# Who rounds the attention weights of steps 1, 27 and 29: VectorE in place of ScalarE, in a graph layer with quadratic attention

## The chip, the cores and the metric

The kernel runs on one core of a Trainium2 chip. The metric is the device time of one execution in microseconds (us), and below it is the median of several executions. The kernel is written by hand in the instruction language: every engine has its own program, and the engines meet at semaphores alone.

## The reference

The layer takes 1250 nodes of 768 features and 20,000 edges. After a layer norm `xn` it adds a graph convolution and an attention without softmax, and behind that a switch feed-forward with 8 experts. What the change touches is the attention, 12 heads of 64:

```python
q, k, v = qkv[0] * SCALE, qkv[1], qkv[2]
A = jnp.einsum('bhnd,bhmd->bhnm', q, k)
numerator = 1.0 + A + 0.5 * A * A
attn = numerator / numerator.sum(axis=-1, keepdims=True)
out = jnp.einsum('bhnm,bhmd->bhnd', attn, v)
```

Since 1 + A + A²/2 = ((1 + A)² + 1)/2, the kernel squares 1 + A on ScalarE, adds 1, and divides by sums that it gets in another way. Products are made in single precision from pairs of rounded numbers: a value is split into a rounded high part (type fp32r) and the low rest, and TensorE multiplies both.

## The kernel before

The twelve heads are done as six pairs, one pass of a loop for each. Five passes run in a hardware loop (`for j in Fori(0, PAIRS - 1)`), the sixth stands behind it (`turn(PAIRS - 1, True)`) without the work for a next pair. A pass has 30 steps: 2 heads by 3 chunks of some 416 queries by 5 pairs of key tiles of 125 nodes. For step `i` in a pass:

- TensorE makes the scores of both key tiles (`MQ` by `KH` and `KL`, lines 1130 and 1131), four matmuls. I call these scores i.
- ScalarE squares 1 + scores into `Pf` (line 815, ACT `Pf<-ps`).
- Either ScalarE (line 793) or VectorE (line 1003) rounds `Pf` + 1 into the high part `Ph`. The list `HI_ON_ACT` (line 593) says which.
- VectorE makes the low part `Pl` = `Pf` + 1 - `Ph` (line 1005).
- Three steps later (`LAG`) TensorE multiplies `Ph` and `Pl` by the values (line 1146, four matmuls). I call this value product i. It waits for `p_lo`, which counts the low parts.

`Pf`, `Ph` and `Pl` are rings of three (`RING`): the square of step i waits for the low part of i-3, and whoever writes `Ph` or `Pl` of step i for value product i-3. VectorE and ScalarE execute what stands in their programs in order. ScalarE issues the rounding of step i-1 behind the square of step i, VectorE does the rounding of step i right ahead of the low part of step i:

```python
if HI_ON_ACT[i]:
    dve.wait_ge(p_hiA, j * NA + (sum(HI_ON_ACT[:i]) + 1))
else:
    dve.wait_ge(sq_done, j * STEPS + (i + 1))
    dve.tensor_scalar(h, f, 1.0, None, ALU.add).then_inc(p_hiD, 1)
    dve.wait_ge(p_hiD, j * ND + (i - sum(HI_ON_ACT[:i]) + 1))
```

Between the steps stands other work, placed by step numbers (`READ_AT`, `TURN_AT`, `FIRST_AT` and the like). What matters here of VectorE's:

- at the start of a pass: lower parts of keys and queries (line 875 `KLB`, line 879 `MA`) and a quadratic form (line 923, `R`), in steps 0 to 9;
- in steps 6 to 22 of the five passes in the loop: 20 comparisons of edge keys (line 958, `eqp`), whose results GpSimd scatters into the matrix `counts` (line 365);
- at the end of a pass: the low part of three groups of transposed keys (line 889, `kt`) at i = 26, 29 and 32, two sums of halves (line 936, `OUN`), and the finish of the pair's output (lines 946, 949, 950, `R`, `OHL`) at i = 30, 32 and 35.

TensorE projects keys and queries for the next pair meanwhile (lines 1873 to 1875, in slices), transposes its keys (line 1069) at i = 24, 27 and 30, where the second and third group wait for VectorE's `kt` of the group before, and at i = 32 makes the Gram matrix of the keys (line 1076), which waits for the third `kt`. Then the next pass begins.

ScalarE at i = 28 has, behind the square of step 28: the rounding of step 27, a copy of half an output (line 802, `tmpo`), a read of queries (line 751, `Q`), the high part of the second key group (line 767, `kt`), then the square of step 29 and the rounding of step 28.

Of the kernel before, what the change touches and what calls it, by code (L numbers as in the profile page):

```python
# [68 lines left out]
STEPS = 30  # L69
# [30 lines left out]
def build(nc, x, src, dst, gnn_w, gnn_b, w_qkv, b_qkv, w_proj, b_proj, sw, sb_, w1, b1, w2, b2, out,  # L100
          counts, keyd, vdram, odram, xfd, x1d, invd):
    ctx = ExitStack()
    with ctx:
# [486 lines left out]
                    pe.wait_ge(xt_lo, FIRST_UNIT[4])  # L590
                value(i)

        HI_ON_ACT = [i % 5 in (1, 3) or i in (0, 27, 29) for i in range(STEPS)]
        NA = sum(HI_ON_ACT)
        ND = STEPS - NA
        FREE = 1
# [140 lines left out]
        def _(act):  # L737
# [48 lines left out]
            def turn(j, last):  # L786
                def round_weights(i):

                    w = step(i)[4]
                    act.wait_ge(sq_done, j * STEPS + (i + 1))  # L790
                    if i >= RING:
                        act.wait_ge(pv_done, j * STEPS + (i - RING + 1))
                    act.activation(Ph[:, i % RING, :, 0:w], Pf[:, i % RING, :, 0:w], ACT.Identity,  # L793
                                   bias=1.0).then_inc(p_hiA, 1)
# [14 lines left out]
                for i in range(END):  # L809
                    if i < STEPS:  # L810
                        w = step(i)[4]
                        act.wait_ge(sc_done, j * STEPS + (i + 1))
                        if i >= RING:
                            act.wait_ge(p_lo, j * STEPS + (i - RING + 1))
                        act.activation(Pf[:, i % RING, :, 0:w], ps[0:T, 2 * (i % 2):2 * (i % 2) + 2, 0:w],  # L815
                                       ACT.Square, bias=1.0).then_inc(sq_done, 1)
                    if 1 <= i <= STEPS and HI_ON_ACT[i - 1]:
                        round_weights(i - 1)
# [40 lines left out]
        def _(dve):  # L859
# [56 lines left out]
            def turn(j, last):  # L916
# [61 lines left out]
                for i in range(END):  # L978
# [15 lines left out]
                    if i < STEPS:  # L994
                        w = step(i)[4]
                        p, f, h = Pl[:, i % RING, :, 0:w], Pf[:, i % RING, :, 0:w], Ph[:, i % RING, :, 0:w]
                        if i >= RING:
                            dve.wait_ge(pv_done, j * STEPS + (i - RING + 1))
# [6 lines that stand above are left out]
                        dve.scalar_tensor_tensor(out=p, in0=f, scalar=1.0, in1=h.bitcast(F32), op0=ALU.add,  # L1005
# [899 lines left out]
```

## Time and profile before

| | |
|---|---|
| median of 3 executions | 1080.57 us (1078.35 to 1081.0) |
| the profiled execution | 1076.3 us, its span 1074.5 us |
| TensorE busy | 928.6 us, 86% of the span |
| VectorE busy | 778.9 us, 72% |
| ScalarE busy | 482.1 us, 45% |
| GpSimd busy | 352.3 us, 33% |
| chain that ended last, by engine | PE 55%, DVE 19%, issue 11%, ACT 6%, DMA 5% |

PE is TensorE's matmuls, PEld its weight loads, DVE VectorE, ACT ScalarE, POOL GpSimd. The six passes lie at 139 to 615 us of the span; a pass in the loop takes 82 us. The span is counted from the first to the last instruction, and the execution's own time is 1.8 us more.

### The profile page before, as it was taken

The page shows a single profiled execution, that of the slowest core. Times are in us where ns is not written, and L with a number is a line of the kernel's source. Part 1 is how long each engine was busy: PE and PEld are TensorE (multiplying, and loading weights), DVE is VectorE, ACT ScalarE, POOL GpSimd, SP SyncE. Part 2 cuts the span into 40 slices and gives each one's busy share as a digit, 9 for nine tenths or more (in the row PEclk, how much of TensorE's full clock was granted, in tenths as well). Part 3 has the DMA queues.
Part 4 walks back from the last instruction along what each step waited for, and adds up shares of the span by engine and source line. Part 5 has one row for each costly group of instructions (what it writes and reads, how often), then busy time and mean ns, then how long its engine had stood idle before and what let it go on. Part 6 is the DMA issues. An engine that isn't in the chain of part 4 may idle for free.

```text
span 1074.5 us, 15640 instructions
## 1 busy us (share of the span) xinstructions
PE 928.6 (86%) x5294; PEld 884.8 (82%) x5294; DVE 778.9 (72%) x1553; ACT 482.1 (45%) x710; POOL 352.3 (33%) x233
## 2 busy tenths in 40 slices
PE   2896799999999999999998679789999996498985
PEld 2896788888888888888887579789999996398885
DVE  6869169888889889889888825665666767467673
ACT  2311266666666766766767402111323223165640
POOL 2025556544545545545345000000000001435562
PEclk9998899999999999999999989989999996589998
DMA  9966452472462462472353194465556533568761
GB/s 278 338 163 152 78 109 19 73 145 29 72 141 33 72 137 36 72 144 29 72 87 91 47 175 119 105 155 145 143 155 159 153 116 130 145 194 265 244 219 46
DMA packets 137406, 136.65 MB, mean 127 GB/s; under 512 B 70361, under 2 KB 118076, under 8 KB 136337
## 3 DMA queue, kind: packets, MB, share of 16 engines
q1 hardware_dynamic: 109550, 119.23, 42.1%
q0 software_dynamic: 27408, 16.66, 10.1%
q8 instruction: 26, 0.43, 0.2%
q10 hardware_dynamic: 403, 0.17, 0.1%
q14 instruction: 19, 0.16, 0.1%
HBM read 94.27 MB, written 38.14 MB: 123 GB/s over the span
## 4 chain that ended last, share of the span: by engine, by line
PE 55%; DVE 19%; issue 11%; ACT 6%; DMA 5%; POOL 1%; SPq 1%; DVEq 0%; ACTq 0%; POOLq 0%
PE ps L1873 13%; PE ps L1874 12%; PE ps L1875 12%; PE ps L1146 6%; DVE Pl L1005 3%; PE ps L1130 3%; PE ps L1131 3%; DVE Ph L1003 3%; DMA out<-oE,ids 2%; ACT Ph L793 2%; ACT Pf L815 2%; PE ps L1512 1%; DVE eqp L958 1%; DMA Cs<-counts 1%; PE ps L1106 1%
## 5 line engine op out<-in xcount | busy, mean ns | idle before, releaser
L365 POOL DMA_INDIRECT counts<-countc,idxu x157 | 269.0, 1713 | 289.8 <-DMA counts<-countc,idxu 197.6
L1005 DVE SCALAR_TENSOR_TENSOR Pl<-Pf,Ph 125x832 fp32r<-125x832 f32 (+1 forms) x180 | 184.0, 1027 | 51.3 <-ACT Ph L793 47.4
L815 ACT ACTIVATE Pf<-ps 125x832 f32<-125x832 f32 (+1 forms) x180 | 156.0, 867 | 129.7 <-PE ps L1131 120.0
L1146 PE MATMUL ps<-Ph,vsb 125*128 125x416 f32 (+1 forms) x360 | 131.2, 365 | 22.6 <-DVE Pl L1005 22.5
L1146 PE MATMUL ps<-Pl,vsb 125*128 125x416 f32 (+1 forms) x360 | 126.7, 352 | 0.0
L1146 PEld LDWEIGHTS ps<-Ph,vsb 125*128 125x128 f32 x360 | 67.7, 188 | 36.0 <-DVE Pl L1005 21.2
L1873 PE MATMUL ps<-wH,XH 128*125 128x384 f32 x240 | 84.3, 351 | 9.9 <-DVE OHL L950 5.8
L1873 PE MATMUL ps<-XH,wqkH 128*128 128x416 f32 (+1 forms) x216 | 83.0, 384 | 9.8 <-DVE wqkL L862 8.1
L1874 PE MATMUL ps<-wL,XH 128*125 128x384 f32 x240 | 83.0, 346 | 0.0
L1875 PE MATMUL ps<-wH,XL 128*125 128x384 f32 x240 | 82.8, 345 | 0.0
L793 ACT ACTIVATE Ph<-Pf 125x832 fp32r<-125x832 f32 (+1 forms) x90 | 80.5, 896 | 0.7
L1874 PE MATMUL ps<-XL,wqkH 128*128 128x416 f32 (+1 forms) x216 | 77.4, 358 | 0.0
L1875 PE MATMUL ps<-XH,wqkL 128*128 128x416 f32 (+1 forms) x216 | 77.3, 358 | 0.0
L1873 PE MATMUL ps<-HH,CH 125*125 125x384 f32 x200 | 69.3, 346 | 7.3 <-DVE CL L1345 7.3
L1146 PEld LDWEIGHTS ps<-Pl,vsb 125*128 125x128 f32 x360 | 68.1, 189 | 0.7
L1874 PE MATMUL ps<-HL,CH 125*125 125x384 f32 x200 | 68.3, 342 | 0.0
L1875 PE MATMUL ps<-HH,CL 125*125 125x384 f32 x200 | 68.3, 341 | 0.0
L1130 PE MATMUL ps<-MA,KHA 128*125 128x416 f32 (+1 forms) x180 | 66.2, 368 | 1.8 <-DVE MA L879 1.8
L1130 PE MATMUL ps<-MB,KHB 128*125 128x416 f32 (+1 forms) x180 | 64.9, 361 | 0.0
L1131 PE MATMUL ps<-MA,KLA 128*125 128x416 f32 (+1 forms) x180 | 63.6, 354 | 0.0
L1651 POOL MEMSET xe<- 105x1536 f32 x1 | 1.4, 1382 | 189.5 <-DVE lg L1349 189.5
L1131 PE MATMUL ps<-MB,KLB 128*125 128x416 f32 (+1 forms) x180 | 63.3, 352 | 0.0
(254 smaller groups left out, 2276.3 us busy)
## 6 DMA issues: line engine op xcount, KB each, us to landing
Cs<-counts SPq DMA_DIRECT2D x20, 546.9 KB
w1s<-L_ffn_w SPq DMA_DIRECT2D x8, 1152.0 KB, 6.1
w2s<-L_ffn_w SPq DMA_DIRECT2D x8, 1152.0 KB, 5.7
odram<-OHL SPq DMA_DIRECT2D x12, 625.0 KB, 7.7
oS<-odram SPq DMA_DIRECT2D x10, 750.0 KB, 4.8
vdram<-VS SPq DMA_DIRECT2D x10, 672.0 KB
vsb<-vdram SPq DMA_DIRECT2D x12, 560.0 KB
kt<-keyd SPq DMA_DIRECT2D x5, 1280.0 KB, 6.0
```

Of the source, the lines that this page charges most:

```text
L365: pool.indirect_dma_start(out=counts, out_offset=bass.IndirectOffsetOnAxis(ap=idxu[:, c:c + 1], axis=0), in_=countc[:, c:c + 1], in_offset ...
L793: act.activation(Ph[:, i % RING, :, 0:w], Pf[:, i % RING, :, 0:w], ACT.Identity, bias=1.0).then_inc(p_hiA, 1)
L815: act.activation(Pf[:, i % RING, :, 0:w], ps[0:T, 2 * (i % 2):2 * (i % 2) + 2, 0:w], ACT.Square, bias=1.0).then_inc(sq_done, 1)
L958: ins = dve.scalar_tensor_tensor(out=eqp[:, s % 2, :], in0=keys_of, scalar=kcur[:, s:s + 1], in1=triw[:, m0:m0 + WINDOW * P], op0=ALU.is_e ...
L1003: dve.tensor_scalar(h, f, 1.0, None, ALU.add).then_inc(p_hiD, 1)
L1005: dve.scalar_tensor_tensor(out=p, in0=f, scalar=1.0, in1=h.bitcast(F32), op0=ALU.add, op1=ALU.subtract).then_inc(p_lo, 1)
L1130: pe.matmul(out_, KH[a][:, kt * T:(kt + 1) * T], q, start=True, stop=False)
L1131: ins = pe.matmul(out_, KL[a][:, kt * T:(kt + 1) * T], q, start=False, stop=True)
L1146: ins = pe.matmul(ps[:, 4 + s % 2, 0:w], vsb[:, 2 * kp + t, a, :], part[:, m % RING, t, 0:w], start=(kp == 0 and t == 0 and part is Ph), s ...
L1873: pe.matmul(out, lh, rh, start=(k == 0), stop=False)
L1874: pe.matmul(out, lh, rl, start=False, stop=False)
L1875: ins = pe.matmul(out, ll, rh, start=False, stop=(k == tiles - 1))
```

## The change

The list that names the steps whose weights ScalarE rounds:

```diff
-        HI_ON_ACT = [i % 5 in (1, 3) or i in (0, 27, 29) for i in range(STEPS)]
+        HI_ON_ACT = [i % 5 in (1, 3) and i != 1 or i == 0 for i in range(STEPS)]
         NA = sum(HI_ON_ACT)
         ND = STEPS - NA
```

Before, ScalarE rounds steps 0, 1, 3, 6, 8, 11, 13, 16, 18, 21, 23, 26, 27, 28, 29 of a pass (15) and VectorE the other 15. Now steps 1, 27 and 29 are VectorE's: 12 and 18, in all six passes. Shapes, buffers and results are the same.

VectorE at the start of a pass in the loop, from the low part of query keys behind step 0 to the low part of step 1:

```order
 L879 TENSOR_TENSOR MA<-Q,MA 64x416
-L1000 REGISTER_ALU
+L1002 ISA
+L1003 TENSOR_SCALAR Ph<-Pf 125x836
+L1004 ISA
 L1005 SCALAR_TENSOR_TENSOR Pl<-Pf,Ph 125x836
 L874 REGISTER_ALU
 L875 TENSOR_TENSOR KLB<-K,KHB 64x418
```

The rounding of step 1 has come in between two instructions of VectorE; the program waits for the square there where it waited for ScalarE's rounding.

VectorE at the end of a pass in the loop, from the keys' low part at i = 26 over the low parts of steps 27 and 28 (left out between) to that of step 29:

```order
 L875 TENSOR_TENSOR KLA<-K,KHA 64x416
+L1002 REGISTER_ALU
+L1003 TENSOR_SCALAR Ph<-Pf 125x2x416
+L1004 REGISTER_ALU
 L1005 SCALAR_TENSOR_TENSOR Pl<-Pf,Ph 125x2x416
...
+L1000 REGISTER_ALU
 L1005 SCALAR_TENSOR_TENSOR Pl<-Pf,Ph 125x2x416
 L889 TENSOR_TENSOR kt<-ps,kt 125x4x128
 L998 REGISTER_ALU
+L1002 REGISTER_ALU
+L1003 TENSOR_SCALAR Ph<-Pf 125x2x416
+L1004 REGISTER_ALU
 L1005 SCALAR_TENSOR_TENSOR Pl<-Pf,Ph 125x2x416
```

Step 27's rounding stands ahead of its low part now, and step 29's between the keys' low part and the last `Pl` of the pass. The register instructions work out the values that the waits compare with; a pass of the loop has 95 of them on VectorE where it had 79.

ScalarE in the same place, behind the squares of steps 28 and 29:

```order
 L815 ACTIVATE Pf<-ps 125x2x416
-L793 ACTIVATE Ph<-Pf 125x2x416
 L802 ACTIVATE tmpo<-ps 64x416
...
 L762 ACTIVATE MA<-Q 64x418
-L793 ACTIVATE Ph<-Pf 125x2x416
 L766 REGISTER_ALU
 L767 ACTIVATE kt<-ps 125x2x128
```

Two roundings are gone, the first of them ahead of everything that ScalarE does up to the rounding of step 28.

## Rows read from the trace of the kernel before

**Rows 1.** third pass: us, busy PE, PEld, DVE, ACT, POOL, clock, DMA share, GB/s

```profile
302.40:384.30 81.90, 76.48 (x405) 71.64 (x404) 71.38 (x138) 54.63 (x80) 45.66 (x27) 1.00 0.46 84
```

**Rows 2.** TensorE's waits, 140 to 630 us: us, times, longest

```profile
PE ps L1146 <- DVE Pl L1005: 22.5, 25, 2.0
PE ps L1069 <- DVE kt L889: 9.4, 8, 1.7
PE ps L1873 <- DVE OHL L950: 5.8, 1, 5.8
```

**Rows 3.** groups by line, 180 to 760 us: busy us, mean ns | idle before

```profile
L1003 DVE TENSOR_SCALAR Ph<-Pf 125x832 fp32r<-125x832 f32 x54 | 33.1, 612 | 4.1 <-DVE eqp L958 1.4 <-PE ps L1146 0.9
L793 ACT ACTIVATE Ph<-Pf 125x832 fp32r<-125x832 f32 x56 | 50.0, 894 | 0.3
```

**Rows 4.** time line, start of the third pass: start, us, engine, instruction [idle before]

```profile
308.82 1.07 DVE L1005 SCALAR_TENSOR_TENSOR Pl<-Pf,Ph 125x836 fp32r<-125x836 f32 x1 [1.10 <-ACT Ph L793]
311.74 1.97 DVE L1005 SCALAR_TENSOR_TENSOR Pl<-Pf,Ph 125x836 fp32r<-125x836 f32 x2
311.75 0.90 ACT L793 ACTIVATE Ph<-Pf 125x836 fp32r<-125x836 f32 x1
312.83 0.46 PE L1146 MATMUL ps<-Ph,vsb 125*128 125x418 f32 x1 [0.90 <-DVE Pl L1005]
```

**Rows 5.** time line, the same pass, step 10

```profile
329.62 0.58 DVE L1003 TENSOR_SCALAR Ph<-Pf 125x832 fp32r<-125x832 f32 x1
330.23 1.03 DVE L1005 SCALAR_TENSOR_TENSOR Pl<-Pf,Ph 125x832 fp32r<-125x832 f32 x1
331.41 0.43 PE L1146 MATMUL ps<-Ph,vsb 125*128 125x416 f32 x1 [1.25 <-DVE Pl L1005]
```

**Rows 6.** time line, the same pass, step 5 on VectorE

```profile
316.24 0.60 DVE L1003 TENSOR_SCALAR Ph<-Pf 125x832 fp32r<-125x832 f32 x1
316.87 1.02 DVE L1005 SCALAR_TENSOR_TENSOR Pl<-Pf,Ph 125x832 fp32r<-125x832 f32 x1
```

**Rows 7.** time line, end of the second pass: VectorE

```profile
291.01 1.03 DVE L1005 SCALAR_TENSOR_TENSOR Pl<-Pf,Ph 125x832 fp32r<-125x832 f32 x1 [1.01 <-ACT Ph L793]
294.24 1.03 DVE L1005 SCALAR_TENSOR_TENSOR Pl<-Pf,Ph 125x832 fp32r<-125x832 f32 x1 [1.46 <-ACT Ph L793]
295.18 0.68 DVE L889 TENSOR_TENSOR kt<-ps,kt 125x512 fp32r<-125x512 f32 x1
295.78 1.02 DVE L1005 SCALAR_TENSOR_TENSOR Pl<-Pf,Ph 125x832 fp32r<-125x832 f32 x1
299.75 0.42 DVE L889 TENSOR_TENSOR kt<-ps,kt 125x256 fp32r<-125x256 f32 x1
```

**Rows 8.** time line, end of the second pass: ScalarE and TensorE

```profile
292.46 0.87 ACT L815 ACTIVATE Pf<-ps 125x832 f32<-125x832 f32 x1
293.20 0.91 ACT L793 ACTIVATE Ph<-Pf 125x832 fp32r<-125x832 f32 x1
290.39 0.35 PE L1131 MATMUL ps<-MB,KLB 128*125 128x416 f32 x1
295.92 0.48 PE L1069 MATMUL ps<-ident,K 128*125 128x128 f32 x2 [1.66 <-DVE kt L889]
300.22 1.46 PE L1076 MATMUL ps<-kt 125*128 125x256 f32 x10
```

**Rows 9.** time line, end of the last pass

```profile
603.71 1.95 DVE L1005 SCALAR_TENSOR_TENSOR Pl<-Pf,Ph 125x832 fp32r<-125x832 f32 x2
606.58 1.96 DVE L1005 SCALAR_TENSOR_TENSOR Pl<-Pf,Ph 125x832 fp32r<-125x832 f32 x2 [0.91 <-ACT Ph L793]
615.47 0.65 PE L1873 MATMUL ps<-wH,XH 128*125 128x384 f32 x1 [5.85 <-DVE OHL L950]
```

**Rows 10.** VectorE's rounding, all 90 (ns min/median/max); GpSimd's last scatter

```profile
L1003 DVE TENSOR_SCALAR Ph<-Pf x90: 532/595/899, 149.0 to 600.5; 125x832 fp32r<-125x832 f32 x60, 125x836 fp32r<-125x836 f32 x30
585.66 1.55 POOL L365 DMA_INDIRECT counts<-countc,idxu  x1 [0.30 <-issue]
```

## The prediction

> **What bounds the kernel now.** I read the busy times by stage first, then TensorE's waits, then the time line around the three steps. In one pass of the loop TensorE is busy 76.5 of 81.9 us at a granted clock of 1.00, VectorE 71.4, ScalarE 54.6, GpSimd 45.7 [rows 1]. So TensorE sets the pace and stands still some 5.4 us a pass. The view of waits says for what: over all passes 22.5 us for low parts `Pl`, 9.4 us for the low part `kt` of transposed keys, 5.8 us once for `OHL` behind the last pass [rows 2]. All three are VectorE's. VectorE is nearly full, and where it stands still it mostly waits for a rounding of ScalarE. A rounding takes ScalarE 894 ns and VectorE 612 ns [rows 3]. So the change gives VectorE 0.6 us of work where it may have been waiting for 0.9 us of ScalarE's. Whether that pays is a matter of each place: what ends the next wait.
>
> The price on VectorE is the spacing from the start of a rounding to the start of its low part: 0.61 us in step 10, 0.63 us in step 5 [rows 5, 6]. I take 0.62.
>
> **Step 1.** VectorE waited 1.10 us for ScalarE before the low part of step 1, so it was free at 308.82 - 1.10 = 307.72 [rows 4]. The square of step 1 was done by then: ScalarE made it ahead of the rounding of step 0, which VectorE had already used. With its own rounding VectorE starts the low part at 307.72 + 0.03 + 0.62 = 308.37, 0.45 us earlier. The two small operations behind it, the rounding of step 2 and the low part of step 2 follow without a wait, 0.45 us earlier as well. TensorE waited 0.90 us for that low part (value product 2, at 312.83 [rows 4]), so it goes on 0.45 us earlier.
>
> But this is lent, not given. The low parts of steps 2 and 3 stand as one row of 1.97 us from 311.74, so it ends at 313.71, and the second, 1.03 us long, starts at 312.68 [rows 4]. ScalarE's rounding of step 3 ends at 311.75 + 0.90 = 312.65 [rows 4]. It follows the squares of steps 3 and 4 and two other operations, and the scores of step 3 come before TensorE's wait, so it doesn't move. VectorE therefore waits 0.45 us there and starts the low part of step 3 when it did before. From there to step 10 VectorE has no wait on another engine that the trace shows, and TensorE's next stop is for the low part of step 10: VectorE ends it at 330.23 + 1.03 = 331.26, and TensorE starts at 331.41 after 1.25 us [rows 5]. That time stays, and the 0.45 us are waited there. The other four passes of the loop and the last have the same stop at step 10. So step 1 is worth 0 in all six passes. What hides it is VectorE's backlog from step 3 to 10; without that it would give 6 x 0.45 = 2.7 us.
>
> **Step 27 in the loop.** VectorE waited 1.01 us before the low part of step 27, so it was free at 290.00 [rows 7]. Its own rounding gives 290.00 + 0.62 = 290.62 against 291.01, about 0.4 us earlier. More matters on ScalarE: with 0.90 us less ahead of it, the square of step 29 moves from 292.46 to 291.56, and the rounding of step 28 from 293.20 to 292.30 [rows 8]. The scores of step 29 are no obstacle, their last matmul ends at 290.39 + 0.35 = 290.74 [rows 8], 0.8 us before. VectorE waited 1.46 us before the low part of step 28 [rows 7], and was free at 292.78, now at 292.4; so the low part starts 0.90 us earlier, at 293.34. The keys' low part moves from 295.18 to 294.28, and TensorE's transposes, which waited 1.66 us for it, from 295.92 to 295.02 [rows 7, 8].
>
> **Step 29 in the loop.** VectorE rounds it behind `kt`, with nothing to hide it: 0.62 us. The low part of step 29 comes at 295.78 - 0.90 + 0.62 = 295.50, 0.28 us earlier. Up to the third `kt` VectorE runs on but for a wait of 0.16 us on itself. That `kt` ended at 299.75 + 0.42 = 300.17, and the Gram matrix started at 300.22 [rows 7, 8], so VectorE is what it waits for. TensorE would be there 0.9 us earlier but gets 0.28. The next pass starts that much earlier, for both engines, since VectorE waits 1 us for step 0 there. The five ends of loop passes show the same waits to 0.1 us. Sum: 5 x 0.28 = 1.4 us gained.
>
> **Steps 27 and 29 in the last pass.** There the square of step 29 waits for the low part of step 26, by the ring of three, and ScalarE's rounding of step 28 comes behind it: neither moves. The rounding of step 27 goes between the two low parts of the row at 603.71, which ends at 605.66; the second then ends at 606.28, still before 606.58 [rows 9]. The idle 0.91 us cover it: 0. The rounding of step 29 goes between the two at 606.58 [rows 9], and from there VectorE runs on through `OHL` to the start of the next stage at 615.47 [rows 9]: 0.62 us lost.
>
> **Small things.** A pass has 16 more register instructions on VectorE. Step 10 has one between rounding and low part already, step 5 none, and the spacings are 0.61 and 0.63 us [rows 5, 6]: I take 0. As an upper bound I take the 0.02 to 0.03 us between the end of a rounding and the start of what waits for it, 16 x 5 x 0.03 = 2.4 us. TensorE's and GpSimd's programs are unchanged, and no DMA moves.
>
> **Sum.** -1.4 + 0.6 = -0.8 us: the profiled execution would take 1075.5 instead of 1076.3 us. It lies 4.3 us under the median of the runs, so for the median I forecast 1080.57 - 0.8 = 1079.8 us. A measurement of this kernel can tell about 0.3% from no change, 3.2 us: this isn't told.
>
> **The rivals.**
>
> *The roundings lie open in the tail (slower).* If the rounding of step 28 does not come earlier, because something else holds ScalarE's square of step 29, then `kt` stays and step 29's 0.62 us go onto VectorE's chain to the Gram matrix in each pass, as they do in the last. 6 x 0.62 = 3.7 us: 1084.3 us; at the longest rounding, 0.90 us, it is 5.4 us. It decides as soon as the gain at step 28 is below 0.62 us. Against it: the 0.8 us that the scores are early. Chance 0.08.
>
> *The tail isn't the last wait (faster).* If TensorE, not `kt`, sets the start of the Gram matrix, each of five passes keeps 0.90 us, and if the backlog at step 10 dissolves too, 0.45 us in six: 4.5 + 2.7 - 0.6 = 6.6 us, 1074.0 us. For it: TensorE is the busiest. Against it: 0.05 us between the end of `kt` and the Gram matrix [rows 7, 8]. Chance 0.08.
>
> *GpSimd holds up VectorE's roundings.* The 90 roundings take 532 to 899 ns [rows 10]; the 14 above 650 ns all overlap one of GpSimd's scatter instructions, of the 36 that overlap none not one is. The excess is 0.3 us at most, and 14 of 54 give 0.06 us on average, which is within my 0.62. If a rounding had to wait for the rest of a scatter instruction, half of 1.55 us [rows 10] in 45.7/81.9 = 0.56 of the cases [rows 1], each would cost 0.43 us more: step 29's gain of 0.28 turns into a loss of 0.15 in five passes, and the sum is 0.8 + 0.6 = +1.4 us, 1082.0 us. Chance 0.12. The Trainium skill's page SBUF — State Buffer, section "SBUF: two separate sides", speaks for this rival: it calls the port pair that VectorE and GpSimd share an exclusive lock, kept for the whole instruction, while the loser fully blocks. The measured excess is smaller than that rule read strictly would give. GpSimd itself could be slowed, but its last scatter starts at 585.66 [rows 10], 30 us before the stage that needs it.
>
> *The register instructions count*: up to +2.4 us, 1082.2 us. Chance 0.10.
>
> **How the numbers follow.** The forecast has the remaining 0.62. Three of the five cases lie within 0.3% (1077.3 to 1083.8 us). Lower end of the range: step 1's 2.7 us stay, 1077.1, less 1.1 us of scatter (the runs differ by 2.65 us): 1076.0. Upper end: 1082.2 plus 1.3 us: 1083.5. Faster by over 0.3%: 0.08 and some scatter, 0.11. Slower: 0.08 and as much, 0.11. Same: 0.78.
>
> **What would show it.** TensorE's wait for the low part of step 2 falls from 0.90 to 0.45 us, and that at step 10 rises from 1.25 to 1.7 us. VectorE's wait before `Pl` of steps 1 and 27 is gone, that before step 28 is about 1 us. TensorE's wait for the second `kt` falls from 1.66 to 1.2 us, and a wait of 0.8 us for the third `kt` appears. The distance from pass to pass falls by 0.3 us, and the last pass ends 0.6 us later against its start. I am wrong if the wait at step 10 stays 1.25 us, if the third `kt` comes later than before, or if the passes change by over 0.5 us.

## The result and the profile after

| | before | the change |
|---|---|---|
| median of 8 executions each, same chip | 1081.43 us (1077.41 to 1085.76) | 1088.81 us (1081.97 to 1095.09) |
| ratio | | 1.0056 [1.0028, 1.0083] |
| the profiled execution | 1076.3 us | 1081.97 us |
| its span, mean granted clock | 1074.5 us, 0.952 | 1080.2 us, 0.942 |

The change is 0.56% slower. The forecast was 1079.8 us and "not told from no change", and the range ended at 1083.5 us. Two further measurements of the same kernel, told below, gave ratios of 1.0012 and 1.0020. In two of the three the interval lies above no change, so there is a loss, but its size differs from one measurement to the next. The ratios and their 95% intervals are worked out from all executions and are not the quotient of the medians. One execution of all that follow, of e5, took 1559.73 us at a mean clock of 0.557, and its ratio and mean clock are those of the other eleven.

First the terms of the forecast, in the order of its steps. The third pass of the change begins at 305.04 us, 2.6 us later than before. Its time line at steps 1 to 3, VectorE and then TensorE's value product of step 2 (start, us, engine, instruction [idle before <-releaser]):

```profile
310.42 0.59 DVE L1003 TENSOR_SCALAR Ph<-Pf 125x836 fp32r<-125x836 f32 x1
311.05 1.03 DVE L1005 SCALAR_TENSOR_TENSOR Pl<-Pf,Ph 125x836 fp32r<-125x836 f32 x1
...
315.49 1.03 DVE L1005 SCALAR_TENSOR_TENSOR Pl<-Pf,Ph 125x836 fp32r<-125x836 f32 x1 [0.54 <-ACT Ph L793]
...
315.01 0.46 PE L1146 MATMUL ps<-Ph,vsb 125*128 125x418 f32 x1 [0.43 <-DVE Pl L1005]
```

The wait of 1.10 us ahead of the low part of step 1 [rows 4] is gone, and TensorE waits 0.43 us at step 2 in place of 0.90. VectorE then waits 0.54 us for ScalarE's rounding of step 3, where the forecast had 0.45. The end of the second pass, VectorE and then TensorE:

```profile
292.90 0.58 DVE L1003 TENSOR_SCALAR Ph<-Pf 125x832 fp32r<-125x832 f32 x1
...
296.27 1.03 DVE L1005 SCALAR_TENSOR_TENSOR Pl<-Pf,Ph 125x832 fp32r<-125x832 f32 x1 [0.98 <-ACT Ph L793]
297.21 0.68 DVE L889 TENSOR_TENSOR kt<-ps,kt 125x512 fp32r<-125x512 f32 x1
297.81 0.58 DVE L1003 TENSOR_SCALAR Ph<-Pf 125x832 fp32r<-125x832 f32 x1
...
302.40 0.42 DVE L889 TENSOR_TENSOR kt<-ps,kt 125x256 fp32r<-125x256 f32 x1
...
297.95 0.48 PE L1069 MATMUL ps<-ident,K 128*125 128x128 f32 x2 [1.19 <-DVE kt L889]
...
302.88 1.46 PE L1076 MATMUL ps<-kt 125*128 125x256 f32 x10 [0.66 <-DVE kt L889]
```

The waits are where the forecast had them. VectorE waits 0.98 us before step 28 (forecast about 1, before 1.46 in [rows 7]), TensorE 1.19 us for the second `kt` (1.2, before 1.66 in [rows 8]), and the Gram matrix has a new wait of 0.66 us (0.8). The last pass takes 71.23 us up to the next stage against 70.89 before, 0.34 us more (forecast 0.62).

One sign came out the other way. In the third pass, which has no disturbance in either kernel, the third `kt` should come earlier in the pass. Time lines of VectorE, the third `kt` before and in the change:

```profile
380.19 0.42 DVE L889 TENSOR_TENSOR kt<-ps,kt 125x256 fp32r<-125x256 f32 x1
...
383.12 0.42 DVE L889 TENSOR_TENSOR kt<-ps,kt 125x256 fp32r<-125x256 f32 x1
```

The pass began at 302.40 before and begins at 305.04 now, so the third `kt` comes after 77.79 us before and after 78.08 in the change, 0.29 us later, and the pass takes 80.72 us where it took 80.44. In the fifth pass it is 0.32 us earlier. Undisturbed passes of the kernel before take 80.44 to 81.28 us, so a term of 0.3 us a pass can't be read from two of them.

TensorE's waits over all passes, 135 to 640 us (in total, times, longest), to set beside [rows 2]:

```profile
PE ps L1146 <- DVE Pl L1005: 20.1, 25, 2.0
PE ps L1069 <- DVE kt L889: 6.4, 7, 1.2
PE ps L1873 <- DVE OHL L950: 5.8, 1, 5.8
...
PE ps L1076 <- DVE kt L889: 3.5, 5, 0.9
```

TensorE waits 2.4 us less for low parts, 3.0 us less at the transposes, and 3.5 us more at the Gram matrix: in sum less than before. And yet the span is 5.7 us longer. Where it went shows when the passes are laid side by side. These are passes 2 to 5 of the change, and the second pass cut up from step 10 (us, busy PE, PEld, DVE, ACT, POOL, clock, DMA share, GB/s):

```profile
221.68:305.04 83.36, 78.13 (x397) 73.07 (x396) 71.80 (x138) 50.84 (x75) 41.03 (x24) 0.96 0.47 79
305.04:385.76 80.72, 75.20 (x397) 70.15 (x396) 72.86 (x139) 50.95 (x75) 43.71 (x25) 1.00 0.47 82
385.76:469.00 83.24, 78.14 (x397) 73.09 (x396) 71.92 (x139) 50.83 (x75) 42.09 (x25) 0.96 0.46 79
469.00:549.72 80.72, 75.11 (x397) 70.12 (x396) 72.52 (x139) 50.83 (x75) 43.94 (x26) 1.00 0.48 82
250.00:252.00 2.00, 1.09 (x8) 1.11 (x8) 2.00 (x4) 1.12 (x2) 1.27 (x1) 1.00 0.10 0
252.00:253.00 1.00, 1.00 (x8) 1.00 (x7) 0.88 (x4) 0.81 (x2) 0.02 (x1) 0.53 0.21 0
253.00:258.00 5.00, 5.00 (x16) 4.76 (x17) 2.52 (x5) 1.15 (x2) 1.65 (x1) 0.50 0.21 20
258.00:259.00 1.00, 1.00 (x8) 1.00 (x6) 0.35 (x1) 0.62 (x1) 0.00 (x0) 0.55 0.35 2
259.00:261.00 2.00, 2.00 (x13) 1.97 (x13) 1.76 (x4) 0.00 (x0) 0.00 (x0) 1.00 0.35 57
```

Passes 3 and 5 take 80.72 us at a granted clock of 1.00. (The stretch of 81.90 us in [rows 1] is not one pass: the third pass before ends at 382.84, and takes 80.44 us. The 82 us told ahead of the prediction are the mean of all five, of which the first takes 86.22.) Passes 2 and 4 hold the same 397 matmuls and take 83.36 and 83.24 us, with 2.9 us more of PE busy time and a clock of 0.96. The finer rows find the place. From 252 to 259 us the granted clock is 0.50, which is 1.2 GHz, the lower of TensorE's two levels, and then it is back at 1.00. TensorE is busy all that time. What it did before stands in its time line:

```profile
250.91 0.43 PE L1146 MATMUL ps<-Ph,vsb 125*128 125x416 f32 x1 [1.84 <-DVE Pl L1005]
...
251.75 1.37 PE L1106 MATMUL ps<-blocks,R 128*125 128x2 f32 x8
...
253.47 0.55 PE L1874 MATMUL ps<-XL,wqkH 128*128 128x416 f32 x1
253.82 0.55 PE L1875 MATMUL ps<-XH,wqkL 128*128 128x416 f32 x1
...
259.49 0.35 PE L1874 MATMUL ps<-XL,wqkH 128*128 128x416 f32 x1
259.68 0.35 PE L1875 MATMUL ps<-XH,wqkL 128*128 128x416 f32 x1
```

It stood still for 1.84 us at the value product of step 10, up to 250.91. Then the same matmuls start 0.35 us apart at the lower level and 0.19 us apart at the higher. The wait was 1.25 us before [rows 5], and the forecast had it grow to 1.7. It did so in every pass of the loop (here 1.76 to 1.90 us), but not in the last, where it is 1.12 us and was 1.16. Behind two of the five it was followed by a fall of the clock; behind 1.90 us in pass 3 it was not:

```profile
334.34 0.43 PE L1146 MATMUL ps<-Ph,vsb 125*128 125x416 f32 x1 [1.90 <-DVE Pl L1005]
```

So the 5.7 us of span are made up as follows. The two passes with a fall are 2.64 and 2.52 us over 80.72, +5.2 us. The rest of the five passes is -0.7 us: they take 414.1 us, 409.0 with the two at 80.72, against 409.7 before (forecast -1.4). The last pass is +0.34, and what lies ahead of the first and behind the last is +0.9. In the execution shown of the kernel before, no pass of the loop has such a fall.

Whole spans of single executions can't be compared as finely as passes. What lies behind the last pass is the same program in all kernels here, and it took 455.3 to 461.6 us in the fourteen profiles, with TensorE at half clock for 77 to 88 us of it.

### The profile page after: what moved, and what is told of

Same layout as the page of the kernel before. It is cut to its first block, busy times and chain, and to the rows that moved or that the text cites. A ratio compares the mean times of both kernels' runs of the same rounds, so it can differ in the third digit from the quotient of the medians.

```text
span 1080.2 us, 15678 instructions
## 1 busy us (share of the span) xinstructions
PE 938.5 (87%) x5294; PEld 894.8 (83%) x5294; DVE 788.2 (73%) x1571; ACT 467.1 (43%) x692; POOL 356.3 (33%) x233
## 4 chain that ended last, share of the span: by engine, by line
PE 54%; DVE 18%; issue 13%; DMA 6%; ACT 5%; POOL 1%; SPq 1%; DVEq 1%; ACTq 0%; POOLq 0%
PE ps L1873 12%; PE ps L1874 12%; PE ps L1875 12%; PE ps L1146 5%; DMA out<-oE,ids 3%; DVE Ph L1003 3%; PE ps L1130 3%; PE ps L1131 3%; DVE Pl L1005 3%; ACT Ph L793 2%; DMA xe<-xfd,ids 1%; PE ps L1106 1%; PE ps L1512 1%; DVE eqp L958 1%; DMA Cs<-counts 1%
## 5 line engine op out<-in xcount | busy, mean ns | idle before, releaser
L365 POOL DMA_INDIRECT counts<-countc,idxu x157 | 274.0, 1745 | 287.4 <-DMA counts<-countc,idxu 212.3
L1003 DVE TENSOR_SCALAR Ph<-Pf 125x832 fp32r<-125x832 f32 (+1 forms) x108 | 66.6, 617 | 4.9 <-DVE eqp L958 1.1
L793 ACT ACTIVATE Ph<-Pf 125x832 fp32r<-125x832 f32 (+1 forms) x72 | 64.5, 896 | 0.6
```

What stands on the lines that cost most here:

```text
L365: pool.indirect_dma_start(out=counts, out_offset=bass.IndirectOffsetOnAxis(ap=idxu[:, c:c + 1], axis=0), in_=countc[:, c:c + 1], in_offset ...
```

## The experiments

Two theories stood at the start. **Clock:** the work is worth what was forecast, and the longer wait at step 10 now and then brings a fall of the clock; then filling that wait with work gets the loss back, though TensorE does more. **Work:** VectorE's three more roundings, or the new wait at the Gram matrix, cost the time; then filling changes nothing or makes it worse. In the expectations, theory A is the first; rival B is the new wait at the Gram matrix, by its length or by falls of its own, and rival C is VectorE's work.

All times are medians, beside runs of the kernel before on the same chip. The mean clock is that of the executions of a row, over their whole span; that of the kernel before was 0.943 over 65 executions in all, and in its profiled execution 0.952.

| kernel | edits | median us (n) | before us | ratio | mean clock |
|---|---|---|---|---|---|
| e1 | step 1 alone | 1083.1 (12) | 1082.84 | 1.0017 [0.9995, 1.0039] | 0.941 |
| e2 | steps 27 and 29 alone | 1079.94 (12) | 1082.84 | 0.9964 [0.9943, 0.9985] | 0.944 |
| e3 | the change, wait at step 10 filled (8) | 1075.18 (6) | 1082.84 | 0.993 [0.9907, 0.9953] | 0.947 |
| e4 | the kernel before, filled (5) | 1077.65 (8) | 1082.84 | 0.995 [0.993, 0.9969] | 0.948 |
| e5 | the change, wait at Gram filled (3) | 1085.86 (12) | 1081.94 | 1.0032 [1.0004, 1.0059] | 0.938 |
| e6 | the change, step 7 to ScalarE | 1076.23 (6) | 1081.94 | 0.994 [0.9917, 0.9964] | 0.945 |
| e7 | 27 and 29, filled (5) | 1073.38 (6) | 1081.94 | 0.9918 [0.9892, 0.9944] | 0.949 |
| e8 | the change again | 1082.8 (12) | 1081.94 | 1.0012 [0.9992, 1.0032] | 0.940 |
| e9 | 27 and 29, step 7 to ScalarE | 1074.73 (6) | 1080.99 | 0.9935 [0.9915, 0.9956] | 0.946 |
| e10 | e9, filled (3) | 1071.59 (6) | 1080.99 | 0.9904 [0.9882, 0.9926] | 0.949 |
| e11 | the change, filled (4) | 1074.99 (6) | 1080.99 | 0.9941 [0.992, 0.9962] | 0.948 |
| e12 | the change a third time | 1082.84 (12) | 1080.99 | 1.002 [1.0001, 1.004] | 0.941 |

### The parts of the change: e1 and e2

e1 moves step 1 alone, e2 steps 27 and 29 alone:

```diff
-        HI_ON_ACT = [i % 5 in (1, 3) or i in (0, 27, 29) for i in range(STEPS)]
+        HI_ON_ACT = [i % 5 in (1, 3) and i != 1 or i in (0, 27, 29) for i in range(STEPS)]
```

```diff
-        HI_ON_ACT = [i % 5 in (1, 3) or i in (0, 27, 29) for i in range(STEPS)]
+        HI_ON_ACT = [i % 5 in (1, 3) or i == 0 for i in range(STEPS)]
```

> Only step 1's rounding goes to VectorE; 27 and 29 stay on ScalarE. Theory A (the clock after the stop at step 10): the 0.45 us of TensorE's wait move from step 2 to step 10, where it stands 1.7 to 1.9 us in one piece, and in some passes the granted clock then falls to 0.50 for 6.8 us, which costs 3 us each time. Expected 3 to 8 us slower than before, with a mean clock of 0.935 to 0.945, and more spread from run to run. Rival B (the tail: the new wait for the third kt brings the clock down or costs the time): no difference from before, within 1 us. Rival C (VectorE simply has too much work): a third of the loss, 2 us, with the clock as before.

> Only steps 27 and 29 go to VectorE; step 1 stays on ScalarE. Theory A: TensorE's wait at step 10 stays 1.25 us, no more falls of the clock than before, and the time is 0 to 2 us below before. Rival B: 5 to 7 us slower, the falls of the clock come with it. Rival C: 4 to 5 us slower with the clock as before.

Steps 27 and 29 make the kernel faster, by 0.36% (1.6 to 6.2 us by the interval), where 0 to 2 us were expected. Step 1 measured 0.17% slower, with an interval that includes no change. That is less than the 3 to 8 us that the clock theory had put on it, and no more than the 2 us of rival C, so e1 by its time alone doesn't tell the theories apart. The waits at step 10 were 1.77 to 1.85 us in e1 and 1.25 to 1.45 in e2. In the profiles e1 had falls behind four of its five waits. The first three passes of e1 by that wait, time lines of TensorE:

```profile
169.79 0.42 PE L1146 MATMUL ps<-Ph,vsb 125*128 125x416 f32 x1 [1.78 <-DVE Pl L1005]
250.57 0.43 PE L1146 MATMUL ps<-Ph,vsb 125*128 125x416 f32 x1 [1.83 <-DVE Pl L1005]
334.52 0.43 PE L1146 MATMUL ps<-Ph,vsb 125*128 125x416 f32 x1 [1.85 <-DVE Pl L1005]
```

e2 shows that a wait as long as the old one can bring a fall too. Its third pass, time line of TensorE:

```profile
330.63 0.43 PE L1146 MATMUL ps<-Ph,vsb 125*128 125x416 f32 x1 [1.25 <-DVE Pl L1005]
```

And windows of e2 ahead of that wait and behind it (columns as in the windows above, the clock is third from the right):

```profile
326.00:330.00 4.00, 3.38 (x18) 2.97 (x16) 3.87 (x10) 3.62 (x6) 1.75 (x2) 1.00 0.14 0
333.00:335.00 2.00, 2.00 (x7) 1.91 (x7) 2.00 (x3) 0.00 (x0) 0.76 (x1) 0.50 0.21 0
```

Three of e2's five passes have such a fall, and the kernel before, with waits of 1.24 to 1.38 us there, has none in the one execution shown. So the length of the wait does not decide it alone, and it is likely that the kernel before loses time in this way as well, only not in the execution that I had read. e4 tests that.

### Filling the wait: e3, e4, e11, and e7

TensorE makes matmuls into a bank that nobody reads at that point, in place of standing still. e3 has 8 on top of the change, e11 4, e4 has 5 on top of the kernel before:

```diff
+                        if m == 10:
+                            pe.wait_ge(r_done, 3 * j + 3)
+                            for _ in range(8):
+                                pe.matmul(ps[:, 6, 0:416], XH[:, 0, 0:P], XH[:, 0, 0:416], start=True, stop=True)
                         pe.wait_ge(p_lo, j * STEPS + (m + 1))
```

> The whole change, and at step 10 TensorE does 8 more matmuls, whose result nobody reads, in the time in which it waits for the low part of step 10. All of the reference's work is done. Theory A: the clock stays at 1.00 in all passes of the loop, and the time is that of before or up to 2 us less. Rivals B and C: no gain over the change, 5 to 8 us slower than before, or more.

> The kernel before, with 5 such matmuls in the wait of 1.25 us at step 10. Theory A: if some executions of the kernel before have falls of the clock at this place too, this one's median is 1 to 4 us below before and its spread smaller; if they never have, it is the same within 0.5 us. Rivals B and C: the same within 0.5 us.

> The whole change with 4 unread matmuls at step 10 instead of 8, so that about 1.0 us of the wait of 1.8 stays open. Theory A: between the change and the change filled, nearer to the filled one: 1075 to 1079 us, mean clock 0.944 to 0.947.

The change with the fill takes 0.993 of the time of the kernel before, with 48 more matmuls. TensorE's time line in e3's second pass:

```profile
249.66 1.75 PE L1146 MATMUL ps<-XH 128*128 128x416 f32 x8 [0.22 <-DVE R L923]
251.25 0.35 PE L1150 MATMUL ps<-Ph,vsb 125*128 125x416 f32 x1
```

Windows of e3 over the same place:

```profile
249.00:252.00 3.00, 2.78 (x15) 2.38 (x14) 2.97 (x6) 2.13 (x3) 0.45 (x1) 1.00 0.19 0
252.00:255.00 3.00, 3.00 (x21) 2.94 (x21) 2.84 (x6) 1.10 (x4) 0.00 (x0) 1.00 0.00 0
```

The wait is gone but for 0.22 us, and the clock stays at 1.00 where the change had 0.50, as it does in all five passes. e3 is 7.7 us below the kernel before, more than the 0 to 2 us expected. Eight matmuls are even too many, since the value product follows them without a wait; half of them (e11) did as well. The kernel before gains too, 0.5% (e4). That bears on a question that the forecast had not asked: why its median lay 4.3 us above the profiled execution. The mean clock over its executions, 0.943, is lower than the 0.952 of the profiled one, and the fill brings the median down to about what the profiled execution took. That its ordinary executions have falls in the loop follows from this gain; no profile of it shows one.

Then the good half of the change and the fill together, e7: steps 27 and 29 on VectorE, five unread matmuls at step 10.

> Steps 27 and 29 on VectorE, step 1 on ScalarE, and 5 unread matmuls in the wait of 1.25 us at step 10. If the 0.45 us of step 1 really are worth nothing, this is the same as the whole change filled: 1075 us, 7 us below before, within 1 us. If they are worth what they first give, it is 2 to 3 us above that.

With the falls in the loop out of the way the terms of the work can be read, from one execution each. Counted from the start of its pass, the second `kt` starts 0.88 to 1.02 us earlier in e7 than in e4 in passes 2 to 5 (forecast 0.90), and the third 0.03 to 0.39 us earlier (forecast 0.28). The five passes take 408.44 us in e4 and 406.86 in e7: 1.6 us, where the forecast had 1.4. But 0.6 us of it lie in the first pass, and e2, with the same three roundings, has 86.22 us there, exactly as before; the other four give 0.95 us.

The last pass takes 70.98 us in e4 and 71.02 in e7, but e4 has a fall of some 3.4 us in the midst of it and e7 has none, so these two don't price the roundings. (Every profile has one more fall at the end of this pass, while TensorE waits for `OHL`.) The nine profiles without a fall in its midst do, though some differ in steps 1 and 7 too: it takes 71.0 to 71.6 us in the seven with steps 27 and 29 on VectorE, and 70.7 and 70.9 us in the two with them on ScalarE (e1, before). That is some 0.5 us, near the 0.62 of the forecast.

In e3 and e11, which have step 1 on top of e7, the five passes take 408.06 and 408.21 us: 1.2 and 1.35 us more than in e7. Half of that is again the first pass, in which e7 is the short one. In the other four it is 0.1 to 0.2 us a pass, less than like passes differ. By the ratios it is 0.1 to 0.2% (0.993 and 0.9941 against 0.9918), within the intervals. So a price of step 1 beyond the falls isn't shown.

### A control: e5

If any work put into any wait helped, the fill at step 10 would prove little. e5 fills the change's other new wait, ahead of the Gram matrix, with three matmuls:

```diff
+                        for _ in range(3):
+                            pe.matmul(ps[:, 0, 0:416], XH[:, 0, 0:P], XH[:, 0, 0:416], start=True, stop=True)
```

> The whole change, and 3 matmuls whose result nobody reads in TensorE's new wait for the third kt, ahead of the Gram matrix, in the five passes of the loop; the wait at step 10 stays open. Theory A (the falls of the clock come from the wait at step 10): 3 to 8 us slower than before, as the change. Rival B (the new wait at the end of a pass brings them): as fast as before or faster, mean clock 0.945 or more.

It is 1.0032 [1.0004, 1.0059], as slow as the change itself. TensorE's waits in e5, 135 to 640 us:

```profile
PE ps L1146 <- DVE Pl L1005: 18.3, 20, 2.0
...
PE ps L1076 <- DVE kt L889: 0.6, 2, 0.3
```

And the place itself, time line of TensorE in e5 at the end of the second pass:

```profile
303.39 0.72 PE L1171 MATMUL ps<-XH 128*128 128x416 f32 x3
304.20 0.86 PE L1076 MATMUL ps<-kt 125*128 125x256 f32 x5
```

The wait at the Gram matrix is filled (0.6 us left of 3.5), the waits at step 10 are still 1.75 to 1.90 us in the loop, and there are three falls behind them. Of the new waits it is the one at step 10 that counts.

### Shortening the wait in place of filling it: e6, e9, e10

The wait at step 10 is VectorE's backlog. e6 takes 0.6 us of it away by giving the rounding of step 7 to ScalarE, on top of the change; e9 leaves step 1 on ScalarE too, and e10 is e9 with three unread matmuls at step 10:

```diff
-        HI_ON_ACT = [i % 5 in (1, 3) and i != 1 or i == 0 for i in range(STEPS)]
+        HI_ON_ACT = [i % 5 in (1, 3) and i != 1 or i == 0 or i == 7 for i in range(STEPS)]
```

```diff
-        HI_ON_ACT = [i % 5 in (1, 3) or i in (0, 27, 29) for i in range(STEPS)]
+        HI_ON_ACT = [i % 5 in (1, 3) or i in (0, 7) for i in range(STEPS)]
```

> The whole change, and in exchange step 7's rounding goes from VectorE to ScalarE, which is idle there. VectorE's backlog from step 3 to step 10 is 0.62 us shorter. Theory A: TensorE's wait at step 10 falls from 1.8 to about 1.2 us; the passes take 0.6 us less each, 3 us in all, and the falls of the clock are as rare as in the kernel before or rarer: 3 to 7 us faster than before. Rival C (VectorE has too much work): only the 3 us of work, 2 us slower to 1 us faster than before.

> A version that might beat both: steps 27 and 29 on VectorE, steps 1 and 7 on ScalarE, no unread matmuls. TensorE's wait at step 10 falls to 0.7 us. Theory A: no falls of the clock in the passes of the loop, mean clock 0.947 or more, 1070 to 1074 us, 8 to 12 us below before. If work alone counts: 3 to 4 us below the kernel with only 27 and 29 moved, 1076 us.

> The same with 3 unread matmuls in the wait of 0.7 us at step 10. Theory A: the short wait brings the clock down rarely, so this is the same within 1 us, or 1 to 2 us faster. If it is 3 us faster or more, even a wait of 0.7 us costs the clock.

e6 has waits of 1.13 to 1.27 us, one fall in its profile, and 0.994, 5.7 us below the kernel before. Some 3 us of that are work, 0.6 us of waiting less in each of five passes; the rest fits rarer falls. e9 has waits of 0.79 to 1.10 us and 0.9935. It was expected 8 to 12 us below the kernel before and without falls; it is 6.3 us below, and 3 us below e2 by the ratios, as much as was expected of the work alone. It has no fewer falls than e6 in its profile: one was there behind 1.10 us in the second pass. TensorE's time line of e9:

```profile
249.62 0.43 PE L1146 MATMUL ps<-Ph,vsb 125*128 125x416 f32 x1 [1.10 <-DVE Pl L1005]
```

Windows of e9 at the wait and behind it, where the clock is 0.57 on average:

```profile
248.00:250.00 2.00, 0.90 (x5) 0.57 (x4) 1.97 (x5) 1.80 (x3) 0.53 (x1) 1.00 0.21 0
251.00:254.00 3.00, 3.00 (x12) 2.87 (x12) 2.84 (x6) 0.53 (x2) 1.25 (x1) 0.57 0.19 0
```

e10 is 3.1 us faster than e9 on the same chip. The intervals overlap a little, but five of e9's six executions are slower than every one of e10's. So even this wait costs more than its length, and e10 is the fastest of all: 1071.59 us, 0.9904 [0.9882, 0.9926]. In its trace the fill and the rest of the wait are:

```profile
248.06 0.73 PE L1146 MATMUL ps<-XH 128*128 128x416 f32 x3
249.04 0.46 PE L1150 MATMUL ps<-Ph,vsb 125*128 125x416 f32 x1 [0.26 <-DVE Pl L1005]
```

### The change again: e8 and e12

> The changed kernel once more, with a second profile. Theory A: TensorE waits 1.8 us at step 10 in each pass of the loop, and falls of the clock begin within some 3 us around the end of that wait and nowhere else in the passes of the loop; 4 to 8 us slower than before. If the falls come at other places, or the loss is there without them, A is wrong.

> The changed kernel a third time, to fix the size: the first comparison gave 1.0056, the second 1.0012. Theory A: 1.001 to 1.005, with a mean clock of 0.936 to 0.941 against 0.943 of before, and the time of an execution falls by 0.4 us for each us less at half clock. A ratio below 0.999 would say that the slowdown was not the change's.

e8 came out less slow than expected, at 1.0012, with an interval that includes no change; e12 is at 1.002, within what was expected. Their waits at step 10 are 1.76 to 2.08 us and their profiles have three falls each, all behind that wait, as in every profile here: no pass of the loop has a fall at another place. The shorter kind of fall is in the third pass of e12, TensorE's time line:

```profile
331.00 0.42 PE L1146 MATMUL ps<-Ph,vsb 125*128 125x416 f32 x1 [1.91 <-DVE Pl L1005]
```

Windows of e12 from the wait on:

```profile
329.00:331.00 2.00, 0.09 (x2) 0.03 (x1) 1.97 (x4) 0.99 (x3) 0.89 (x1) 1.00 0.20 0
331.00:334.00 3.00, 3.00 (x18) 2.95 (x19) 2.84 (x7) 1.89 (x3) 2.15 (x2) 0.90 0.00 0
334.00:335.00 1.00, 1.00 (x5) 0.94 (x4) 1.00 (x2) 0.00 (x0) 1.00 (x1) 0.50 0.42 1
335.00:337.00 2.00, 2.00 (x9) 1.92 (x7) 0.85 (x3) 1.12 (x2) 1.00 (x1) 0.55 0.27 7
```

It lasts some 3.4 us where that of the change lasts 6.8, and such a pass takes 82.2 to 82.3 us, where one without a fall takes 80.15 in e12 and 80.72 in the change: 1.5 to 2.1 us. Over the three measurements the change has 32 executions, with a median of 1083.3 us, against 1081.9 us in 73 of the kernel before. Their mean clocks are 0.940 and, over the 65 for which it is known, 0.943. Among the 32, time and clock go together (correlation -0.89): 0.94 us for each 0.001 of mean clock. The mean clock counts every stage, so it doesn't say how much of this lies in the loop: of the 21.5 us at half clock that the profile of the change has more than that of the kernel before, 13.7 are the two falls and 7 lie behind the last pass.

## Why the prediction was wrong

**The step that failed** is the last of step 1: "That time stays, and the 0.45 us are waited there. [...] So step 1 is worth 0 in all six passes." The first half is right. But I treated 0.45 us of waiting at step 2 and 0.45 us more at step 10 as the same thing. At step 10 they lengthen a pause of 1.25 us to 1.8. I counted TensorE's waits as time and never asked what a pause does to the clock of the work behind it; a granted clock of 1.00 in [rows 1] was read as a property of the stage. What the runs showed in its place: in the profile of the change, TensorE ran at half clock for 6.8 us behind two of the five longer stops, and the two passes took 2.64 and 2.52 us more, 5.2 of the 5.7 us; with the stop filled the same change is at 0.993 (e3). The profiles of the five kernels that keep step 1 on VectorE without a fill or a shorter wait (the change, e1, e5, e8, e12) have 25 waits of 1.75 to 2.08 us, and 15 are followed by a fall. The 20 waits of 0.79 to 1.45 us (before, e2, e6, e9) have 5, and the 25 places with a fill (e3, e4, e7, e10, e11) none. A count from one execution each is no law.

Length alone is not the cause. The stop for the second `kt` was 0.79 to 1.66 us long, 70 times in the fourteen profiles, 15 of them at 1.63 to 1.66 ([rows 8] has one), and no fall followed any. What stands around the two stops differs: behind the one at step 10 come four matmuls and then eight with only two columns each (L1106, 1.37 us in the lines above), behind the one at the transposes come two of 128 columns and then matmuls of 416. No run changed this neighbourhood and left the stop, so whether it counts stays open. And in the last pass, falls of 3.4 us stand behind a stop of 2.0 us at a later step in five profiles (e3, e4, e5, e10, e11), four of them of filled kernels: the fill removes the falls of its own stop alone.

**The median of the kernel before.** "It lies 4.3 us under the median of the runs" was added as a constant. For the most part it was this effect, as far as e4 shows: the profiled execution has no fall in the loop, and filling the stop takes 5.2 us off the median. The stretch behind the last pass, which varies by 6.3 us from profile to profile, can have a share in it.

**Steps 27 and 29 in the loop:** right in the mechanism. The second `kt` came 0.88 to 1.02 us earlier and the third 0.03 to 0.39 (forecast 0.90 and 0.28; e7 against e4), and the three waits at the pass end came out within 0.15 us. The sum, forecast 1.4 us, measured 1.6 with the falls away, 0.95 of it in passes 2 to 5.

**The last pass:** +0.62 us forecast, +0.34 measured in the change, some 0.5 over the nine profiles told above. Right, within what such numbers can tell. That the stop at step 10 would grow in this pass too was wrong (1.12 us, before 1.16).

**The price of a rounding:** the 108 roundings on VectorE take 617 ns on average, where [rows 3] had 612 for a part of them; the median is 595 ns in both. This group of the page, change:

```profile
L1003 DVE TENSOR_SCALAR Ph<-Pf 125x832 fp32r<-125x832 f32 (+1 forms) x108 | 66.6, 617 | 4.9 <-DVE eqp L958 1.1
```

**The rivals.** The open tail is out: the second `kt` comes 0.9 us earlier and the third doesn't come later (e7 against e4). That the tail isn't the last wait is out: the Gram matrix starts 0.06 us behind `kt` (302.40 + 0.42 to 302.88). GpSimd's hold and the register instructions had the slower side, but neither fits: undisturbed passes got no longer (80.72 us, before 80.44 to 81.28), and a fill on TensorE, which touches neither, got the loss back. The right mechanism was not among them.

**Open.** Why a wait is followed by a fall in one pass and not in the next, with the same length, and at one place and not at another. Why the first eight executions had a lower mean clock (0.937) than the 24 later ones (0.941). And why the change in the first measurement is slower than e1 and e2 add up to (1.0017 and 0.9964 would give 0.998, e8 and e12 measured 1.001 and 1.002). That the falls in the loop need the pause at step 10 is shown by taking it away, in five kernels, and by the control e5; what in the pause or around it sets it off wasn't separated.

## What to carry to other kernels

A wait that is moved isn't always neutral on TensorE: two stops at two places and one longer stop of the same sum can be different things, since a stop may be followed by some microseconds at half clock. Here that hung on the place as well as on the length. So before calling a shift free, look how long the longest single stop of TensorE becomes, and read the granted clock behind such stops, in more than one execution. A median well above the profiled execution, at a lower mean clock, is a hint that falls are there; it doesn't say in which stage. Where the stop can't be removed, a few unread matmuls in it are cheap: they gained 0.5% on the kernel before, and with steps 27 and 29 on VectorE and step 7 on ScalarE 1.0%.

## What the runs showed that I had not expected

- TensorE's clock fell to half behind stops of 1.1 to 2.1 us, in passes in which it was busy 93% of the time. Behind the stops for the second `kt`, up to 1.66 us long in the same passes, it never did. Each fall lasted some 3.4 or 6.8 us and cost 1.5 to 2.1 us or 2.5 to 3.2 us of the pass. The Trainium skill (TensorE: Matmul & The Clock Gate, section "HAM oscillation — how this bites in real kernels") warns of falls for idle gaps longer than any of these stops; by that rule alone none of these stops would have cost more than its own length, with which the traces don't agree. The next section of that page, "A second HAM failure mode: psum-queue depth-cycling", tells of a kernel whose clock went up and down though TensorE stood still only briefly between groups of matmuls; these traces agree with that one in so far as falls follow stops of 1.1 us.
- The fall does not begin with the stop, but when TensorE is at work again: the wait ended at 250.91 us, the clock was 1.00 up to 252 us and 0.50 from 253. In the 20 falls of the loop it began 0.2 to 2.4 us behind the end of the stop.
- Doing more work on the busiest engine made the kernel faster, with 18 matmuls (e10) to 48 (e3) more.
